# Three rounds of message passing over a gathered table: waits folded, shared and moved

## What is computed

```python
ew = (edge_weight - edge_weight.min()) / (edge_weight.max() - edge_weight.min() + 1e-08)
def rgcn(x, W, root, bias):
    m = sum_r mask_r * (x[src] @ W[r]) * ew          # per edge
    return segment_sum(m, dst, N) + x @ root + bias
h = relu(layernorm(x))
x = x + rgcn(relu(rgcn(h, W1, root1, b1)), W2, root2, b2)
h = relu(layernorm(x))
out = x + segment_sum(edge_weight * h[src], dst, N) @ W.T + b
```

## Time and profile before

| | us |
|---|---|
| median of three timed runs (7032.99 to 7052.95) | 7034.69 |
| the profiled execution, its own time | 7006.04 |
| its span, first to last instruction | 7004.2 |
| POOL busy | 4430.2 |
| PE busy | 2575.8 |
| DVE busy | 1368.6 |
| ACT busy | 443.4 |

### The profile page before, as it was taken

How to read it: one execution, slowest core, us unless ns; L and a number is a source line. 1 busy time by engine, 2 the same in 40 slices (tenths; PEclk the granted TensorE clock), 3 DMA queues, 4 the chain that set the end, 5 groups by cost and what they waited for, 6 DMA issues and landing times.

```text
span 7004.2 us, 38158 instructions
## 1 busy us (share of the span) xinstructions
PE 2575.8 (37%) x11399; PEld 2399.4 (34%) x11399; DVE 1368.6 (20%) x5032; ACT 443.4 (6%) x1183; POOL 4430.2 (63%) x4697
## 2 busy tenths in 40 slices
PE   1444444444444433233333333332333333333334
PEld 1433434433434333233333223332333333333333
DVE  4322222222222211111111111111111111111111
ACT  3100100100000000000000000000000000000000
POOL 4566656656665656666666666665666666666665
PEclk8777767777777765555555555555555555555555
DMA  4222222222222211112111212121222222222221
GB/s 128 55 59 59 59 57 57 61 58 60 60 58 58 59 50 51 52 51 53 52 52 52 52 51 54 52 52 46 53 53 52 52 52 52 51 53 52 52 53 48
DMA packets 264696, 391.05 MB, mean 56 GB/s; under 512 B 81547, under 2 KB 176920, under 8 KB 264488
## 3 DMA queue, kind: packets, MB, share of 16 engines
q0 software_dynamic: 150048, 307.60, 17.4%
q1 hardware_dynamic: 114440, 80.97, 3.8%
HBM read 336.91 MB, written 51.34 MB: 55 GB/s over the span
## 4 chain that ended last, share of the span: by engine, by line
another core or an unknown queue 63%; issue 11%; PE 11%; DVE 11%; DVEq 1%; ACT 1%; DMA 1%; POOL 0%; SPq 0%; ACTq 0%
PE bank L777 5%; DVE acc L965 3%; DVE win L1050 3%; PE bank L746 3%; DVE bank L1080 3%; PE bank L672 1%; DVEq L957 1%; PE bank L692 1%; PE bank L720 1%; DVE stats L848 0%; ACT tile_T L496 0%; POOL rows L376 0%; DMA h_rows<-table 0%; DVEq L965 0%
## 5 line engine op out<-in xcount | busy, mean ns | idle before, releaser
L376 POOL DMA_INDIRECT rows<-table,idx x4625 | 4366.9, 944 | 2533.6 <-issue 1423.8
L777 PE MATMUL bank<-win,rows 128*128 128x48 f32 x6252 | 1411.2, 398 | 671.6 <-issue 613.4
L777 PEld LDWEIGHTS bank<-win,rows 128*128 128x128 f32 x6252 | 1407.7, 330 | 614.6 <-issue 553.4
L965 DVE TENSOR_TENSOR acc<-acc,bank 128x48 f32 x1173 | 236.6, 202 | 3702.9 <-remote 2985.9
L746 PE MATMUL bank<-win,rows 128*128 128x192 f32 x3126 | 678.0, 372 | 554.7 <-DVE win L1050 401.6
L746 PEld LDWEIGHTS bank<-win,rows 128*128 128x128 f32 x3126 | 612.3, 223 | 584.6 <-DVE win L1050 423.3
L1050 DVE TENSOR_SCALAR win<-iota,key,sw_col 128x192 f32<-128x192 f32 x1563 | 502.3, 388 | 1.2 <-issue 1.0
L718 PE MATMUL bank<-ident,tile_T 128*128 128x128 f32 x98 | 46.2, 474 | 1206.3 <-ACT tile_T L496 1111.5
L720 PE MATMUL bank<-W3T,tile_T 128*128 128x128 f32 x196 | 77.6, 500 | 1115.9 <-ACT tile_T L496 989.3
L718 PEld LDWEIGHTS bank<-ident,tile_T 128*128 128x128 f32 x98 | 18.2, 186 | 1259.9 <-ACT tile_T L496 1155.8
L720 PEld LDWEIGHTS bank<-W3T,tile_T 128*128 128x128 f32 x196 | 49.2, 312 | 1167.6 <-ACT tile_T L496 1030.8
(11 more groups left out here) (103 smaller groups left out, 1091.3 us busy)
## 6 DMA issues: line engine op xcount, KB each, us to landing
rows<-table,idx POOLq DMA_INDIRECT x4625
table<-st SPq DMA_DIRECT2D x147, 256.0 KB
x_rows<-table SPq DMA_DIRECT2D x49, 128.0 KB
x_rows<-in_x_dram SPq DMA_DIRECT2D x48, 128.0 KB
h_rows<-table SPq DMA_DIRECT2D x48, 128.0 KB
out_dram<-st SPq DMA_DIRECT2D x48, 128.0 KB
acc<-in_x_dram SPq DMA_DIRECT2D x13, 448.0 KB, 3.7
table<-acc SPq DMA_DIRECT2D x13, 448.0 KB
```

The costliest lines, as they stand in the source:

```text
L376: eng.indirect_dma_start(out=rows[:, slot, :], out_offset=None, in_=table[:, :], in_offset=bass.IndirectOffsetOnAxis(ap=idx[:, slot:slot + ...
L777: ins = eng.matmul(agg_ps[v][:, q * W:(q + 1) * W], rows[:, slot, :], window[:, slot, :], start=(k == 0), stop=(k == n - 1))
L965: eng.tensor_tensor(a, a, sums_ps, ALU.add).then_inc(s_acc, 1)
```

## The change

It does six things, and computes the same.

- Slots share semaphores in pairs (`rows_signal`): both gathers of a pair count the same one up, and PE waits once, at the even chunk, for both (`wait_rows`). The chunks of the last unit have one each (`s_tail`).
- Waits that another wait implies are dropped: `s_acc` at PE's unit start in rounds 1 and 2, `s_own_sb` of own_turn, `s_acc` of the mix, `s_own0_add` of own0, `s_fin_a` and `s_fin_d` of the finishes, `s_mix` of the copies on ACT, and others like them.
- Second waits are put on instructions that had none. PE in round 0 waits for `s_wide` of the next group at the second chunk of the present one, and for `s_sums` at the last chunk of a half. In rounds 1 and 2 `s_window` of the next unit is waited for at the second chunk of the unit's last group. DVE in round 0 waits for `s_own0_add` and `s_own0` at the windows of groups 1 and 2, and in round 2 for its stores and loads ahead of loading the bases.
- In round 0 PE mixes unit u-1 before it transposes h, ACT does `own_out` before `wide_out`, and DVE does add_own0(u-1) ahead of group 3's windows.
- In rounds 1 and 2 DVE takes the indices ahead of the four adds, and weighs windows behind the second and the fourth.
- Nothing but `s_idx` bounds how far POOL runs ahead, as before.

Instructions with more than one wait fall from many hundreds to a few dozen: as the order counts them there are 1708 further waits on PE before and 81 after, on DVE 756 and 46, on ACT 902 and 16. 2436 records that only wait are gone.

```diff
-        s_row = [sem(f"s_row{k}") for k in range(NSLOT)]
+        s_row = [sem(f"s_row{k}") for k in range(NSLOT // 2)]
+        s_tail = [sem(f"s_tail{k}") for k in range(last_chunks)]
...
+        def rows_signal(u, k):
+
+            return s_tail[k] if u == NU - 1 else s_row[(u % RING * UC + k) // 2]
+
+        def wait_rows(eng, r, u, k):
+
+            if u == NU - 1:
+                eng.wait_ge(s_tail[k], 16 * (r + 1))
+            elif k % 2 == 0:
+                v = u % RING
+                per_round = NI if v < last_units - 1 else NI - 1
+                eng.wait_ge(s_row[(v * UC + k) // 2], 32 * (r * per_round + u // RING + 1))
...
             def wide_in(t, s):
 
                 eng.wait_ge(s_prep, t + 1)
-                if not isinstance(t, int) or t < NT - 2:
+                if not isinstance(t, int):
                     wait(eng, s_fin_a, t)
                 eng.matmul(wide_of(t)[:, :], tile_T[:, s, :], W2s[:, :, :].rearrange("p r d -> p (r d)"),
...
                 elif first(t, 2):
                     eng.wait_ge(s_fin_a, 2 * NT)
-                wait(eng, s_fin_d, t + ((r - 1) * NT - 1))
+                    wait(eng, s_fin_d, t + (NT - 1))
+                elif not isinstance(t, int):
+                    if r == 1:
+                        eng.wait_ge(s_fin_a, t + (NT - 1))
+                    eng.wait_ge(s_fin_d, t + ((r - 1) * NT - 1))
                 if r == 1:
                     eng.transpose(fin_of(t, s)[:, 0:D], tile_T[:, s, :], ident[:, :]).then_inc(s_fin, 1)
...
                         if q in groups_of(u):
                             n = group_chunks(u, q)
                             g = u * UG + q
-                            eng.wait_ge(s_wide, g + 1)
-                            if q % 2 == 0:
-                                wait(eng, s_sums, u * 2 + (h - 3))
-                            if first(u, RING):
-                                eng.wait_ge(s_norm, g + 1)
+                            raw = first(u, RING)
                             for k in range(n):
-                                if not first(u, RING):
-                                    slot = v * UC + q * CG + k
-                                    eng.wait_ge(s_row[slot], i * 16 + (row_base(0, slot) + 16))
+                                if not raw:
+                                    wait_rows(eng, 0, u, q * CG + k)
+                                if k == 0 and (raw or g == RING * UG):
+                                    eng.wait_ge(s_wide, g + 1)
+                                    if q % 2 == 0:
+                                        wait(eng, s_sums, u * 2 + (h - 3))
+                                    if raw:
+                                        eng.wait_ge(s_norm, g + 1)
+                                if k == 1 and not raw and g < NG - 1:
+                                    eng.wait_ge(s_wide, g + 2)
+                                if k == n - 1 and not raw and q % 2 == 1 and g < NG - 1:
+                                    eng.wait_ge(s_sums, (u + (q == 3)) * 2 + ((h + 1) % 2 - 3))
                                 ins = eng.matmul(half_ps[v % 2 * 2 + h][:, q % 2 * RW:(q % 2 + 1) * RW], rows[:, v * UC + q * CG + k, :],
                                                  wide[:, v % 2, q * CG + k, :], start=(k == 0), stop=(k == n - 1))
                             if q % 2 == 1 or q == groups_of(u)[-1]:
                                 ins.then_inc(s_half, 1)
                         if q == 1:
-                            own_turn(i, u, v)
                             if not first(u, 1):
                                 mix_unit(u - 1, v - 1, UG)
+                            own_turn(i, u, v)
                     own0(u, v % 2)
...
 
                 def unit(i, v):
                     u = i * RING + v
-                    eng.wait_ge(s_window, u * 2 + ((r - 1) * 2 * NU + 2))
-                    if not first(u, RING) or r > 1:
-                        eng.wait_ge(s_acc, u * UG + (r * NG - (RING - 1) * UG) if not first(u, RING) else r * NG)
+                    if u < RING:
+                        if r > 1:
+                            eng.wait_ge(s_acc, r * NG)
+                        eng.wait_ge(s_window, u * 2 + ((r - 1) * 2 * NU + 2))
                     for q in groups_of(u):
                         n = group_chunks(u, q)
                         for k in range(n):
                             slot = v * UC + q * CG + k
-                            eng.wait_ge(s_row[slot], i * 16 + (row_base(r, slot) + 16))
+                            wait_rows(eng, r, u, q * CG + k)
+                            if k == 1 and q == UG - 1 and RING - 1 <= u < NU - 1:
+                                eng.wait_ge(s_window, u * 2 + ((r - 1) * 2 * NU + 4))
                             ins = eng.matmul(agg_ps[v][:, q * W:(q + 1) * W], rows[:, slot, :], window[:, slot, :],
                                              start=(k == 0), stop=(k == n - 1))
...
             def add(r, g, base, sums_ps):
 
                 a = acc[:, bass.ds(base, W)]
-                wait(eng, s_acc, g + r * NG)
+                if r > 0 or g % UG or g < RING * UG:
+                    wait(eng, s_acc, g + r * NG)
                 eng.tensor_tensor(a, a, sums_ps, ALU.add).then_inc(s_acc, 1)
 
             def add_own0(t):
 
                 a = columns(t)
-                eng.wait_ge(s_own0, t + 1)
+                if not isinstance(t, int) or t == NT - 1:
+                    eng.wait_ge(s_own0, t + 1)
                 eng.tensor_tensor(a, a, own0_ps[:, 0:P], ALU.add).then_inc(s_own0_add, 1)
 
...
+                            for k in range(0, n, 2):
+                                wait_rows(eng, 0, u, q * CG + k)
                             mean_and_var(NB + g, p, [rows[:, v * UC + q * CG + k, :] for k in range(n)])
                         if n:
                             if q == 0 and not first(u, 2):
                                 eng.wait_ge(s_half, u * 2 - 2)
+                            if q == 1 and not first(u, RING):
+                                eng.wait_ge(s_own0_add, u - 1)
+                            if q == 2 and not first(u, 1):
+                                eng.wait_ge(s_own0, u)
+                            if q == 3 and not first(u, 1):
+                                eng.wait_ge(s_acc, u * UG)
+                                add_own0(u - 1)
                             for k in range(n):
                                 c = u * UC + (q * CG + k)
                                 ins = eng.tensor_scalar(wide[:, v % 2, q * CG + k, :], iota[:, 0:RW], key0[:, bass.ds(c, 1)],
@@ -1058,7 +1102,7 @@
                             take_idx(src_col, u * UC + (RING - 1) * UC, (v - 1) % RING, chunks_of(u + RING - 1))
                         if q == 2 and not first(u, 1):
                             adds(u - 1, v - 1, UG)
-                        if q == 3 and not first(u, 1):
+                        if q == 3 and not n:
                             eng.wait_ge(s_acc, u * UG)
                             add_own0(u - 1)
...
                     n = chunks_of(u + RING) if ahead else 0
                     c = u * UC + RING * UC
+                    if r == 2 and u > 1 and u % 2 == 0:
+                        stored_out(u - 2)
+                    elif r == 2 and u > 0:
+                        loaded_x2(u - 1)
                     base = bases(u, len(groups_of(u)))
                     if not first(u, 2):
                         finish(u - 2, (u - 2) % XR, (u - 2) // XR)
                     eng.wait_ge(s_agg, u + ((r - 1) * NU + 1))
+                    if ahead:
+                        take_idx(code, c, v, n, r)
                     for q in groups_of(u):
                         add(r, u * UG + q, base[q], agg_ps[v][:, q * W:(q + 1) * W])
-                        if ahead and q == 0:
-                            take_idx(code, c, v, n, r)
-                        if ahead and q in (1, 2):
-                            weigh(c, v, q - 1, n, u + RING)
+                        if ahead and q % 2 == 1:
+                            weigh(c, v, q // 2, n, u + RING)
 
                 def finish(t, v, n):
                     if r == 1:
```

56 lines of the change are left out of this document (31 added, 25 removed).

## The result

The changed kernel took 7153.99 us in the median of four runs (7146.32 to 7167.06), the kernel before 7038.07 beside it (7032.99 to 7052.95): a ratio of 1.0163, 95% interval 1.014 to 1.0186. It is slower, by 116 us where I had forecast 55.

What follows compares the result with a forecast made beforehand. No engine is full: POOL's gather stream (5861 us floor) plus its waits for indices behind PE's late completions bound the kernel. -15 + 67 + 3 = +55 gave 7090 us; likeliest case's own range 7042 to 7170, overall 6800 to 7250.

Steps and rivals of the forecast that it cites:

- a property of the stream: PE's completions arrive late while POOL streams its gathers and at once when it pauses; the change does not touch this.
- Waits dropped, records gone: Implied or moved waits on PE, DVE and ACT: cost 0, being passed before or during longer waits for PE.
- the bound of 8 a unit: If dropped waits did count: 2436 records over 3 x 98 units, 8 a unit, at most 1.2 us a unit.
- Slots in pairs: PE's even chunk waits for both gathers and starts up to 1.25 us later: cost 0.
- Rounds 1 and 2: -15: DVE's indices ahead of the four adds gain 0.12 to 0.21 us in 94 waits: 11 to 20 us, taken as -15.
- The wait one group ahead and add_own0: Round 0: three chunks of group 2 (1.81 us) and add_own0 (0.42 us) join the chain in 30 long waits: +67 us.
- s_own0 at group 2's windows: Round 0, DVE's wait for PE after the COPY of the indices: 0 to 0.4 us, behind POOL's restart.
- the +2.23 us: Lengthening of the round-0 chain in each of 30 long waits, 1.81 plus 0.42 us.
- the units between +3: Round-0 units that pause less: the chain is ahead of need, three are within 3 us of it, +1 us each.
- Relief: Rival: PE's lateness depends on its waits and records, so fewer shorten POOL's waits; about 6590 to 6950 us, chance 0.31.
- The doubled chain: Rival: late s_own0 holds group 2's windows in round 0, adding 5.9 us in 30 waits, 177 us: 7267 us.
- chain twice or more pauses: Heading for the doubled-chain rival or more frequent pauses: 7170 to 7270 us, chance 0.13.

Runs made afterwards that it cites:

- before_few_rows: The kernel before with each table gather fetching 64 rows instead of 128 (result not the reference's): 7007.79 us in a single run, beside 7017.38.
- before_more_waits: The kernel before with one more, already fulfilled wait on each matmul of rounds 1 and 2: 7042.15 us, ratio 1.0022.
- after_slot_rows: The changed kernel with one semaphore for each of the 64 slots again: 7126.65 us, ratio 1.0156 to the kernel before.
- before_wide_rows: before_wide_ahead with the slots' semaphores in pairs added: 7095.43 us, ratio 1.0112 to the kernel before.
- before_wide_ahead: The kernel before with only PE's round-0 wait for s_wide moved one group ahead, to the second chunk: 7088.53 us against 7027.94, ratio 1.0088.
- before_own_ahead: The kernel before with DVE's add_own0 ahead of group 3's windows and s_own0 waited for at group 2's: 7033.2 us, ratio 1.0013.
- before_wide_own: The kernel before with the edits of both before_wide_ahead and before_own_ahead: 7097.61 us against 7022.22, ratio 1.0104.

## Why the prediction was right or wrong

- **What bounds the kernel.** POOL's stream and PE's late completions: that both are there is read rightly for this chip. That the lateness is "a property of the stream" is wrong: two other chips have the stream without it. And before_few_rows shows that with it POOL's stream is not the floor of rounds 1 and 2.
- **Waits dropped, records gone: 0.** before_more_waits bears it out for the records (+0.2% for 3126 more). Whether dropping the waits shifts the rhythm is open. The traces hold 2391 fewer records that only wait, where I had counted 2436; the bound of 8 a unit stays.
- **Slots in pairs: 0.** after_slot_rows and before_wide_rows put it at 0.07% and 0.24%, neither clear of noise.
- **Rounds 1 and 2: -15.** Right, if a little small. In the six other kernels on chips 13 and 5 that keep the old order in rounds 1 and 2, with all rows and no added waits, a round takes 2229 to 2232 us from first gather to last; in the four with the indices ahead (the changed kernel's own profile left out) 2217 to 2221. That is 11 a round, some 23 together. The profile of before, with 2219 and 2220, is the odd one out, which is why its pair with the changed kernel shows only 9.
- **The wait one group ahead and add_own0: +67.** Measured 2.28 us longer a pause x 30 = 68 in the profiles; alone +61 (before_wide_ahead) and +5 (before_own_ahead). The weight loads of the seven chunks took 4.12 us in the mean of the 45 pauses, those of the four before 2.36 in the mean of 30: 1.75 us more where I had 1.81. In 23 of the 45 pauses they took 4.34 us. In the pause shown they took 3.71: the granted clock was 0.50 of full speed (the lower level) from their begin, behind 13 idle us, and 1.00 from 1639.6 on. The first add came 0.3 us later, which I had not forecast, and makes up for what the parts fell short by.
- **s_own0 at group 2's windows: 0 to 0.4.** It waited 2.58 us, but in a unit with room, and costs nothing alone.
- **The sum: +55.** The step that failed is the count by which the +2.23 us was multiplied. I kept 30 long pauses and gave the units between +3. The changed kernel has 45, which adds 195 us and takes 99 us of short pauses away: +96 in the profiles' terms, where I had 3. The parts that I had priced do come to my sum where they are tested without the rest: +75 for both moves of round 0 (before_wide_own) and -23 for rounds 1 and 2 are +52. The other 60 us or so of the 116 come only with the rest of the change, and why it brings them is open. The hint was in the trace: before, the long pauses came irregularly with shorter ones between, so a longer chain could change the rhythm and not only the length. I had priced more frequent pauses only in the range of a rival, at 0.13.
- **Rivals.** Relief fell. The doubled chain, through s_own0, isn't what happened, and its range of 7170 to 7270 doesn't hold the time, though the heading under which I gave it, "chain twice or more pauses", names what did happen. The range of 6800 to 7250 held 7154, and my likeliest case's own range of 7042 to 7170 did too. That was luck: its upper end stands for group 1 being delayed as well, which didn't happen, and it leaves the -15 and the +3 of the sum out.

What stays open: which of the remaining parts (dropped waits, s_sums at the last chunk, ACT's order, or the moves together) turns 27 to 30 long pauses into 45, some 0.6% of the time; and what on chips 13 and 5 holds PE's completions back.

## What to carry to other kernels

A wait that is moved to an earlier instruction to save a record makes all work from there on depend on it: look at which instructions then stand behind the latest event in the stretch that sets the pause, and multiply by how often, not only by how long. Work that doesn't depend on a late event belongs ahead of it in the queue: putting all windows of a unit ahead of the adds, with the indices moved too, gave 1.8%, where the change with all its saved waits lost 1.6%. Before a trace's stall is taken for a property of the kernel, the same program should be seen on another chip, and a count from one profile should be held beside that of a second execution of the same code.

## What the runs showed that I had not expected

The same program took 7154 us on one chip and 5901 on another, at the same 1.25 us a gather and nearly the same mean granted clock (0.569 and 0.592). On the first, PE's completions reach the other engines 10 to 31 us behind their records while POOL streams, and its trace holds 18379 records of increments; on the other it is 0.5 us, with 87326 such records. With late completions, a gather 4% faster shortened nothing that one run could show: the pauses grew by what the gathers gained.
